# Attention scores from two fp16 parts with on-chip power-of-two scales, in place of three bf16 parts

## The reference, cut to what matters

```python
q = (hidden_states @ Wq).reshape(b, s, N_HEADS, HEAD_DIM)      # 16 heads of 16
k = (hidden_states @ Wk).reshape(b, s, N_KV_HEADS, HEAD_DIM)   # 4 heads of 16
v = (hidden_states @ Wv).reshape(b, s, N_KV_HEADS, HEAD_DIM)
q, k = _apply_rope(q, position_ids), _apply_rope(k, position_ids)
scores = jnp.einsum('bshd,bthd->bhst', q, k) * scale           # scale = 1/4
attn = jax.nn.softmax(scores, axis=-1)
out = jnp.einsum('bhst,bthd->bshd', attn, v)
...
weights, sel = jax.lax.top_k(probs, TOP_K)                     # routing by row, needs exact scores before it
```

## Time and profile before

| | before |
|---|---|
| median of 3 runs | 431.02 us (430.18 to 434.71) |
| profiled execution, span from first to last instruction | 458.5 us |
| PE busy | 423.1 us, 92% |
| DVE busy | 318.8 us, 70% |
| ACT busy | 247.3 us, 54% |
| POOL busy | 152.9 us, 33% |
| start to first row maximum | 0 to 26.4 us |
| maxima alone | 26.4 to 52.1 us |
| 64 steps of attention | 52.1 to 224.3 us |
| routing and experts | to 458.5 us |

### The profile page before, as it was taken

One profiled execution on the slowest core, in us unless ns is written; L12 is line 12 of the kernel. 1 busy time (PEld: TensorE's weight loads), 2 busy tenths in 40 slices (PEclk: granted clock), 3 DMA queues, 4 the chain that ended last, 5 costly groups with the idle time before them and its releaser, 6 DMA issues.

```text
span 458.5 us, 9187 instructions
## 1 busy us (share of the span) xinstructions
PE 423.1 (92%) x3449; PEld 224.7 (49%) x3449; DVE 318.8 (70%) x739; ACT 247.3 (54%) x406; POOL 152.9 (33%) x177
## 2 busy tenths in 40 slices
PE   8999899999999999999999998987879878979995
PEld 4555323333333333333577776654545545646673
DVE  6878998999999999943476995464544343345457
ACT  1566678788878888887735254333123223233062
POOL 3068201220303030301210008565655764655400
PEclk9999999999999999999999999989979988999998
DMA  8500000000000000000110762488977886896192
GB/s 270 214 4 2 1 1 2 0 2 1 0 1 1 1 1 2 1 1 0 47 36 12 244 245 67 155 283 297 305 258 257 272 299 206 285 286 227 39 375 76
DMA packets 20535, 54.81 MB, mean 120 GB/s; under 512 B 4513, under 2 KB 8825, under 8 KB 20491
## 3 DMA queue, kind: packets, MB, share of 16 engines
q1 hardware_dynamic: 16075, 45.81, 29.5%
q0 software_dynamic: 4416, 8.41, 5.4%
HBM read 49.74 MB, written 8.13 MB: 126 GB/s over the span
## 4 chain that ended last, share of the span: by engine, by line
PE 63%; DVE 12%; another core or an unknown queue 8%; issue 7%; ACT 4%; DMA 4%; POOL 1%; SPq 0%; POOLq 0%; DVEq 0%; ACTq 0%
PE PM L1379 13%; PE EP L1628 7%; PE EP L1366 6%; PE M L1332 6%; PE EP L1369 6%; PE PM L1332 3%; PE EP L1481 3%; PE PM L1650 2%; PE PM L1661 2%; PE EP L1287 2%; DMA w<-ychoice 1%; ACT w L750 1%; PE EP L1303 1%; DMA wide<-in_wmod 1%
## 5 line engine op out<-in xcount | busy, mean ns | idle before, releaser
L670 ACT ACTIVATE QS<-EP 128x1024 f32<-128x1024 f32 x128 | 124.1, 1022 | 24.9 <-PE EP L1369 24.4
L853 DVE TENSOR_REDUCE mx<-M 128x1 f32<-128x512 f32 x171 | 111.6, 684 | 7.2 <-PE M L1332 4.2
L1628 PE MATMUL EP<-w,QS 128*128 128x352 f32 (+1 forms) x244 | 69.9, 497 | 0.0
L1379 PE MATMUL PM<-QS,VA 128*32 128x512 f32 x512 | 68.2, 605 | 0.0
L723 ACT ACTIVATE OT<-EP 128x176 f32<-128x176 f32 x46 | 14.7, 319 | 95.4 <-PE EP L1628 80.6
L853 DVE TENSOR_REDUCE mx<-PM 128x1 f32<-128x512 f32 x85 | 58.1, 684 | 3.8 <-PE M L1332 3.6
L1332 PE MATMUL M<-KT,QT 64*128 64x512 bf16 x171 | 51.4, 384 | 0.2 <-ACT QTB L625 0.2
L1366 PE MATMUL EP<-QT,KT 64*128 64x512 bf16 x256 | 49.0, 377 | 1.0 <-ACT QT L585 0.5
L1369 PE MATMUL EP<-QTB,xh 34*128 34x512 bf16 x256 | 48.9, 377 | 0.0
L525 POOL DMA_INDIRECT QS<-h2rows,tab x26 | 28.6, 1099 | 44.9 <-DVE tab L1073 37.2
L1481 PE MATMUL EP<-segu,QSB 128*128 128x352 f32 x128 | 41.0, 463 | 0.3 <-issue 0.2
(11 more groups left out here) (288 smaller groups left out, 607.3 us busy)
## 6 DMA issues: line engine op xcount, KB each, us to landing
w<-in_w SPq DMA_DIRECT2D x61, 544.0 KB
w<-ychoice SPq DMA_DIRECT2D x8, 512.0 KB, 7.4
segu<-in_segu SPq DMA_DIRECT2D x1, 1408.0 KB, 10.0
x<-in_x SPq DMA_DIRECT2D x2, 512.0 KB, 4.9
wide<-in_wmod SPq DMA_DIRECT2D x1, 1024.0 KB, 7.4
h2rows<-qkv SPq DMA_DIRECT2D x2, 512.0 KB, 2.9
out<-x SPq DMA_DIRECT2D x8, 128.0 KB, 2.3
sedn<-in_sedn SPq DMA_DIRECT2D x1, 640.0 KB, 10.9
```

The lines of the kernel that those rows point to most:

```text
L670: nc.scalar.activation(PT[n % 3][:, 2 * p:2 * p + 2, :], EP[p][:, :, :], ACT.Exp, scale=HD ** -0.5).then_inc(e_done, 1)
L853: nc.vector.tensor_reduce(out=mx[:, u % 2, q, j, c:c + 1], in_=src, axis=AX.X, op=ALU.max).then_inc(m_free, 1)
L1379: ins = mm(PV[HP * j:HP * j + HP, :], VA[:, tt, g, :], PT[n % 3][:, j, :], start=tt == 0, stop=tt == NT - 1)
L1628: ins = mm(BANK[b][lo:lo + n, 0:I13], XGT[b][:, c * P + lo:c * P + lo + n], w[:, r, c * I13:(c + 1) * I13], start=c == 0, stop=c == NC - 1)
```

## The change

The values are scaled so that two fp16 parts hold q and k. POOL squares the weights and the modulation (`squares`), PE multiplies them into a bound on the size of q and k (line 1280 after), DVE takes the largest and makes powers of two from its exponent (`scales`), and ACT multiplies by them as it copies qkv out of PSUM, now in two instructions for each tile (q columns, then k and v columns), with the scale as a pointer to a column. The exponential takes its scale by pointer too. Queries are kept as high, low, high and keys as high, high, low (48 rows), and two more rows carry the maximum, divided by 2^14 on POOL in an instruction of its own; the key side holds 2^14 there.

```diff
-        QK = [(0, "K", 0, 0), (0, "Q", 0, 0), (0, "Q", 0, 2), (0, "K", 0, 2), (0, "Q", 0, 4), (0, "Q", 0, 6),
-              (1, "K", 0, 0), (1, "K", 0, 2), (0, "K", 1, 0), (0, "K", 1, 2), (1, "K", 1, 0), (1, "K", 1, 2),
-              (1, "Q", 0, 0), (1, "Q", 0, 2), (1, "Q", 0, 4), (1, "Q", 0, 6)]
-        QK_COUNT, MOD_AT = (6, 6, 8, 8, 10, 12, 13, 15, 16, 16), (1, 1, 2, 3, 4, 4, 5, 6)
+        QK = [(0, "K", 0), (0, "Q", 0), (0, "Q", 2), (0, "K", 2), (0, "Q", 4), (0, "Q", 6),
+              (1, "K", 0), (1, "K", 2), (1, "Q", 0), (1, "Q", 2), (1, "Q", 4), (1, "Q", 6)]
+        QK_COUNT, MOD_AT = (6, 6, 8, 8, 8, 8, 9, 11, 12, 12), (1, 1, 2, 3, 4, 4, 5, 6)
...
+            def squares():
+                pool.wait_ge(ld_qkv, 16)
+                qk_cols = wqkv[:, :, 0:(NH + NG) * HD]
+                pool.tensor_tensor(w_sq[:, :, :], qk_cols, qk_cols, ALU.mult)
+                pool.wait_ge(s_modc, 1)
+                pool.tensor_tensor(mod_sq[:, :, :], modc[:, 0:2, :], modc[:, 0:2, :], ALU.mult).then_inc(s_sq, 1)
+                pool.wait_ge(s_sq, 1)
+                pool.tensor_tensor(mod_rep[:, :, :], mod_sq[:, 0, :].unsqueeze(2).to_broadcast([P, NC, P]),
+                                   mod_sq[:, 1, :].unsqueeze(2).to_broadcast([P, NC, P]), ALU.add).then_inc(s_sq, 1)
+            inverse_root(0)
+            squares()
+            inverse_root(1)
...
             def minus_max(u):
...
                 pool.wait_ge(s_neg, u + 1)
-                pool.tensor_copy(part[:, :, :, BM], negm[:, u % 2]).then_inc(s_negh, 1)
+                pool.tensor_tensor(part_m[:, u % 2], negm[:, u % 2], down[:, :, :], ALU.mult).then_inc(s_part, 1)
+                pool.wait_ge(s_part, u + 1)
+                pool.tensor_copy(part[:, :, :, MR_ROWS], part_m[:, u % 2]).then_inc(s_negh, 1)
                 pool.wait_ge(s_negh, u + 1)
-                pool.tensor_tensor(part[:, :, :, BM + 1], negm[:, u % 2], part[:, :, :, BM], ALU.subtract).then_inc(s_negm, 1)
+                pool.tensor_tensor(part[:, :, :, MR_ROWS + 1], part_m[:, u % 2], part[:, :, :, MR_ROWS], ALU.subtract).then_inc(s_negm, 1)
...
-                nc.scalar.activation(qkv[:, t, :], BANK[(7 + t) % 8][:, 0:QKV], ACT.Copy).then_inc(s_qkvev, 1)
+                if t == 0:
+                    act.wait_ge(s_scale, 1)
+                for i, cols in enumerate((slice(0, NH * HD), slice(NH * HD, QKV))):
+                    ins = nc.scalar.activation(qkv[:, t, cols], BANK[(7 + t) % 8][:, cols], ACT.Copy, scale=powf[:, i:i + 1])
+                ins.then_inc(s_qkvev, 1)
...
-                    nc.scalar.activation(PT[n % 3][:, 2 * p:2 * p + 2, :], EP[p][:, :, :], ACT.Exp, scale=HD ** -0.5).then_inc(e_done, 1)
+                    nc.scalar.activation(PT[n % 3][:, 2 * p:2 * p + 2, :], EP[p][:, :, :], ACT.Exp, scale=exp_scale[:, 0:1]).then_inc(e_done, 1)
...
+            def scales():
+                dve.wait_ge(s_bound, 1)
+                nc.vector.reduce_max(bound[:, 0:1], BANK[6][:, 0:NH * HD], AX.X)
+                then(nc.vector.reduce_max(bound[:, 1:2], BANK[6][:, NH * HD:(NH + NG) * HD], AX.X))
...
                 for i in range(2):
-                    rows = slice(AR * i, AR * i + AR)
-                    mm(EP[p][:, i, :], KT[rows, g, keys], QT[rows, 2 * g + p, queries], start=True, stop=False)
-                for i in range(2):
-                    rows = slice(AR * i, AR * i + BR)
-                    ins = mm(EP[p][:, i, :], KTB[rows, g, keys], QTB[rows, u % 2, p, :], start=False, stop=True)
+                    rows = slice(AR * i, AR * i + SR)
+                    ins = mm(EP[p][:, i, :], KT[rows, g, keys], QTB[rows, u % 2, p, :], start=True, stop=True)
                 ins.then_inc(e_fill, 1)
```

More of the change, by code:

```diff
@@ L328, in qk_evac @@
         def qk_evac(item, bank):
-            h, kind, part, j = item
-            dst = QT if kind == "Q" else (KT, KTB)[part]
+            h, kind, j = item
+            dst = QT if kind == "Q" else KT
             return (dst[:, j:j + 2, 512 * h:512 * h + 512],
-                    bank.bitcast(bf16).rearrange("p (j s) -> p j s", j=2))
+                    bank.bitcast(f16).rearrange("p (j s) -> p j s", j=2))
         @block.sync
@@ L407, in _, with inverse_root @@
             pool.tensor_copy(identb[:, :], ident[:, :]).then_inc(s_ident, 1)
+            pool.tensor_copy(identh[:, :], ident[:, :]).then_inc(s_ident, 1)
             pool.memset(VA[:, :, :, :], 0.0).then_inc(s_va, 1)
-            pool.wait_ge(s_va, 1)
-            pool.memset(VA[:, :, :, HD:HD + 1], 1.0).then_inc(s_va, 1)
+            pool.memset(down[:, :, :], 1.0 / CEIL).then_inc(s_minus1, 1)
             pool.memset(sedn[0:P - SLAST, NSC - 1, :], 0.0).then_inc(s_pad, 1)
-            for h in range(2):
+            def inverse_root(h):
                 pool.wait_ge(s_const, 3)
@@ L613, in _ @@
             later_mod(0)
-            qk(8)
-            qk(9)
-            act.wait_ge(s_qs, 2)
-            nc.scalar.activation(q_part(HALVES[1], 1), q1, ACT.Copy).then_inc(s_qs, 1)
-            for n in range(10, len(QK) - 1):
+            for n in range(8, len(QK) - 1):
                 qk(n)
@@ L806, in _ @@
                     nc.vector.tensor_scalar(modc[:, 1, :], BANK[0][:, NC:2 * NC], 1.0, None, ALU.add).then_inc(s_modc, 1)
+                else:
+                    scales()
                 dve.wait_ge(s_rstd, h + 1)
                 normalise(h, xh, s_h, 2)
+            then(nc.vector.tensor_scalar(power[:, 2:4], power[:, 0:2], -1.0, float(254 * 2 ** 23), ALU.mult, ALU.add))
+            nc.vector.scalar_tensor_tensor(out=exp_scale[:, :], in0=powf[:, 2:3], scalar=HD ** -0.5, in1=powf[:, 3:4],
+                                           op0=ALU.mult, op1=ALU.mult).then_inc(s_exps, 1)
             dve.wait_ge(ld_rope, 32)
@@ L1252, in _ @@
             pe.wait_ge(s_modc, 1)
+            pe.wait_ge(s_sq, 2)
+            for c in range(NC):
+                ins = mm(BANK[6][:, 0:(NH + NG) * HD], mod_rep[:, c, :], w_sq[:, c, :], start=c == 0, stop=c == NC - 1)
+            ins.then_inc(s_bound, 1)
             def later_mod(i):
@@ L1269, in transpose_qk @@
             def transpose_qk(item, bank, done):
-                h, kind, part, j = item
-                b = bank.bitcast(bf16)
+                h, kind, j = item
+                b = bank.bitcast(f16)
                 if kind == "Q":
-                    pe.wait_ge(*((s_qs, 3) if h else (s_split, 4)))
+                    pe.wait_ge(*((s_qs, 2) if h else (s_split, 4)))
                 else:
-                    pe.wait_ge(*((s_kb, h + 1) if part else (s_k1, 3) if h else (s_split, 4)))
+                    pe.wait_ge(*((s_k1, 2) if h else (s_split, 4)))
                 for i in range(2):
@@ L1279, in transpose_qk @@
                         if kind == "Q":
-                            parts = [QSA[:, 4 * h + t, 2 * (j + i) + n // 2, 0:BM] for n in range(4)]
-                        elif part == 0:
-                            parts = [KSA[:, 4 * h + t, j + i, HD * (n % 2):HD * (n % 2) + BM] for n in range(4)]
+                            parts = [QR[:, 4 * h + t, 2 * (j + i) + n // 2, 0:2 * HD] for n in range(4)]
                         else:
-                            parts = [KSB[:, 4 * h + t, j + i, :]] * 2
+                            parts = [KR[:, 4 * h + t, j + i, :]] * 2
                         n = P // len(parts)
                         for m, src in enumerate(parts):
-                            ins = tr(b[n * m:n * m + n, o:o + P], src, identb[:, :])
+                            ins = tr(b[n * m:n * m + n, o:o + P], src, identh[:, :])
                 ins.then_inc(done, 1)
@@ L1338, in transpose_B @@
                 pe.wait_ge(s_negm, u + 1)
-                b = fill(a_free).bitcast(bf16)
+                b = fill(a_free).bitcast(f16)
                 for j in range(2):
```

137 lines of the change are left out of this document (68 added, 69 removed).

## The result

The change makes the kernel slower by 1.3%: 437.8 us (median of 4 runs, 436.5 to 439.8) against 431.25 us for the kernel before beside it, ratio 1.0132 with a 95% interval of 1.0082 to 1.0182. A second series gave 437.74 against 432.4 us, 1.0122 (1.0092 to 1.0151). The forecast was 431.4 us, range 425.5 to 435.5.

What follows compares the result with a forecast made beforehand. A loop of PE fill, output and DVE reduction, 2.49 us a step, bounds steady attention, not PE alone. Terms 0 + 2.45 - 1.8 - 1.8 + 1.5 = +0.35 us on the 431.02 us median give 431.4 us, range 425.5 to 435.5.

Steps and rivals of the forecast that it cites:

- the sum: Whole kernel: steady steps, POOL link, maxima alone, last steps and start add up to +0.35 us.
- rival C: Attention steps: less PE work lowers the granted clock, +1.5 us a step; twenty slow steps give 461 us; chance 5%.
- signs of being wrong: Attention: steps shorter than 2.45 us, PE waiting no longer for DVE, or a clock below 1.
- from three slow steps on: Steady attention steps, under rival C: three steps at the lower clock cost 4.5 us, over 1%.
- Steady steps: About 48 of 64 attention steps: 0.43 us less PE work each is hidden behind DVE; price 0.
- Third link on POOL: Chain to the maximum's transpose: a third POOL instruction costs 0.35 us in each of seven units, +2.45 us.
- Maxima alone: Stretch 26.4 to 53.4 us, before attention: fewer key transposes and less score work give -1.8 us.
- My reading of the stalls: Maxima alone: DVE's stalls next to the key transposes, largest 0.65 us at 39.85, sum to about 1.4 us.
- Start: Before the first reduction: POOL's squares holding DVE (+1.3), split qkv copies (+0.25) and DVE's splits sum to +1.5 us.
- End, -1.8 and one link of +0.35: Last ten attention steps, without maxima: less score work gives -1.8 us; one POOL link costs 0.35 us.
- my slots: Last ten steps: 0.43 us off for each of three steps and 0.22 at each end, -1.7 us.
- Routing: Routing and experts: nothing changes, 0; gains ahead are carried to the end one for one.

Runs made afterwards that it cites:

- x2: Kernel after with 3 filler matmuls (results unread) in each of the four places where key transposes stood before: 437.21 us, ratio to before 1.0105.
- x3: As x2, plus 4 filler matmuls in each of the first two steps of attention, ahead of the output: 436.37 us, ratio to before 1.0097.
- x10: Kernel after with each pair of score matmuls issued twice into the same place: 440.16 us.
- x13: Kernel after with squares on ACT, the maximum's parts on DVE, fillers ahead of the first scores, none in attention's first two steps: 429.45 us, ratio to before 0.9936.
- x4: Kernel before with the second (34-row) matmul of each score left out, key transposes kept: 429.24 against 431.87 us, ratio 0.9957.
- x6: Kernel after with the maximum's division by 2^14 and split as two DVE instructions instead of three on POOL: ratio to before 1.0041.
- x8: Kernel before without its six filler matmuls in steps 4 and 5 of the maxima alone, key transposes kept: ratio 0.999.
- x11: Kernel after with the exponentials' scale as a constant instead of a pointer to a column: 439.24 us.

## Why the prediction was wrong

**The step that failed** is that the sum holds the clock at 1.00 and has nothing for its fall; that was left to rival C. I saw that less work on PE could lower the clock, looked for it in the steady step alone ("no gap in a step would be over 0.6 us"), and gave it 5%. In the steady steps the clock did stay at 1.00. It fell from 41 to 50 us, where the change took transposes away, and from 58 to 61 us, where PE stands for ACT and DVE. That is one of the signs of being wrong that the prediction named (a clock in attention below 1). I had even listed the four transposes that go, and priced them as pure gain. The argument against C was a busy share (8.50 of 10 from 50 to 60 us); after shows 0.57 of the clock with PE 97% busy, so that share said nothing. And "from three slow steps on" priced the fall in steps of the steady loop, not in stages that DVE paces. Shown by x2 and x3: 2.6 us.

For the first fall the cause is shown: matmuls put back in the places of the transposes (x2) keep the clock. For the second it is shown that more matmul work there or ahead of it ends it (x3, x10, x13). Which part of the change brings it is open: x2, with the first fall mended, still has it, and x4, which takes half of the score work from the kernel before, has not.

By the other steps:

- **Steady steps, 0:** right. The steps stay 2.49 us; score work taken away (x4) or doubled (x10) leaves the units as they were. The wait for DVE grew by less than the 0.43 a step that I gave, since part of the waiting is now for ACT.
- **Third link on POOL, +2.45:** right, and x6 shows the cause. Five units +1.75, the sixth +0.72: 0.37 of it is more than a link, goes away in x6, and no run explains it. Not priced: ACT's copy of the queries comes later as well, and the fill behind it waits 0.36 us (75.51 us).
- **Maxima alone, -1.8:** did not come. (The sum as written, -1.4 + 0.1 - 0.43, is -1.73.) The 40 reductions take 28.25 us instead of 26.98. With the clock held (x2) they take 26.36, 0.6 less than before. But x2's twelve fillers take PE's time in the very places, so no run shows what the removal gives by itself at a clock of 1.00. My reading of the stalls was loose as well: the largest went with the fillers in x8, while all transposes stood.
- **Start, +1.5:** right, 1.21 where the clock held (1.18 counted from the modulation). Not seen: PE stands behind DVE there, and in three of seven profiles the clock falls there, another 1.2 to 1.6 us. As x8, without the squares, has such a fall too, it is not shown that the change brings it. By the Trainium skill, SBUF — State Buffer, "SBUF: two separate sides", the port pair of DVE and GpSimd is an exclusive lock that the first one holds for its whole instruction, where DVE is in a 2-port mode or has two inputs in SBUF. No run shows whether the normalising is of these kinds, but the trace agrees beside POOL's 1.27 us: there the four take 2.61 us, 1.24 more than alone. Beside its 0.65 us they take 1.66, only 0.29 more, which does not show a full hold.
- **End, -1.8 and one link of +0.35:** -1.18. x4, with neither pointers nor the link, gains 1.9 there, and x11 gives the pointers 0.35, which closes the sum: -1.9 + 0.35 + 0.35 = -1.2. I had put the pointers' price too low: my slots sum to -1.7, and the -1.8 has nothing for the pointers.
- **Routing, 0:** +0.32, unexplained, gone in x6. Together with the 0.37 of the last unit it is 0.7 us that the sum did not have.

Without the clock's 2.6 us the marks sum to +3.1, 434.1 us, which is still inside the range; the clock put the result outside. Even so the forecast of 431.4 us would have been 2.7 us off, 2.0 of it the gain of the maxima that did not come. The rule that I had cited under C, that the throttled state is the default and activity releases it (the Trainium skill, TensorE: Matmul & The Clock Gate, "What's actually happening"), was the right warning: x2 (clock 1.00 from 40 to 52 us instead of 0.57), x3 and x13 agree with it.

## What to carry to other kernels

When a change takes work from PE, read the granted clock for every stage from which a matmul or transpose goes, the short ones too, and ask what PE still does there; its busy share doesn't tell, since slow matmuls look busy. Price a removed instruction as a loss as well as a gain until a row or a run excludes it. A helper instruction on POOL can cost what DVE loses beside it, and a chain of three small instructions costs its links each time a ring waits for it: move it to an engine that is free, or to the one whose result it takes.
